# Ten probability tiles a pair through device memory in place of eight, five differences of them on GpSimd, and new instruction orders

## What is computed

```python
Q = (x @ Wq.T).reshape(b, n, H, R)          # H = 8, R = 64
K = (x @ Wk.T).reshape(b, n, H, R)
V = (x @ Wv.T).reshape(b, n, H, d)          # d = 128
attn = jax.nn.softmax(jnp.einsum('bnhr,bmhr->bhnm', Q, K), axis=-1)
out = jnp.einsum('bhnm,bmhd->bnd', attn, V) # summed over the heads
x = _layernorm(x + out)
h = jax.nn.silu(_tlin(x, w1_w, w1_s)) * _tlin(x, w2_w, w2_s)
h = gelu(_tlin(h, h1_w, h1_s)); h = gelu(_tlin(h, h2_w, h2_s))
x = _layernorm(x + _tlin(h, w3_w, w3_s))
```

## Time and profile before

| | |
|---|---|
| median of three executions | 941.37 us (940.90 to 941.87) |
| the profiled execution | 942.06 us, with a span of 940.3 us from the first to the last instruction |
| period of a pair, steady | 56.7 us |
| PE busy | 915.1 us, 97% |
| ACT busy | 841.1 us, 89% |
| DVE busy | 819.9 us, 87% |
| POOL busy | 590.4 us, 63% |
| mean granted TensorE clock | 0.994 |

### The profile page before, as it was taken

One profiled execution on the slowest core, in us unless ns is written; L12 is line 12 of the kernel. 1 busy time (PEld: TensorE's weight loads), 2 busy tenths in 40 slices (PEclk: granted clock), 3 DMA queues, 4 the chain that ended last, 5 costly groups with the idle time before them and its releaser, 6 DMA issues.

```text
span 940.3 us, 19462 instructions
## 1 busy us (share of the span) xinstructions
PE 915.1 (97%) x6071; PEld 766.8 (82%) x6071; DVE 819.9 (87%) x1786; ACT 841.1 (89%) x2081; POOL 590.4 (63%) x587
## 2 busy tenths in 40 slices
PE   8989999999999999999999999999999999999996
PEld 6887888878888888888888888888888888888886
DVE  7999698897989989898897989989898897987767
ACT  7969998999989899999999999999999999989963
POOL 7954655748567485665847557485665747565753
PEclk9999999999999999999999999999999999999998
DMA  6005042241423315143151423415143141420010
GB/s 205 13 22 171 13 144 82 76 138 46 149 66 112 115 32 169 47 141 96 49 155 53 150 69 92 129 39 160 55 135 102 49 152 49 132 82 23 24 35 25
DMA packets 113640, 84.49 MB, mean 90 GB/s; under 512 B 11264, under 2 KB 93824, under 8 KB 113536
## 3 DMA queue, kind: packets, MB, share of 16 engines
q1 hardware_dynamic: 113536, 83.22, 28.3%
HBM read 45.69 MB, written 37.49 MB: 88 GB/s over the span
## 4 chain that ended last, share of the span: by engine, by line
PE 63%; DVE 16%; ACT 9%; DMA 5%; issue 5%; SPq 1%; POOL 1%; POOLq 0%; DVEq 0%; ACTq 0%
PE bank L1717 11%; PE bank L1718 11%; PE bank L1584 9%; PE bank L1585 7%; PE bank L1586 7%; PE bank L1590 7%; PE bank L1644 7%; ACT prob L661 6%; DVE pt_lo L316 4%; DVE t_lo L316 2%; DVE neg_max L1086 2%; DMA crossing<-prob 2%; DMA pt_lo<-crossing 2%; DVE gated L1170 2%; DVE gated L1162 2%
## 5 line engine op out<-in xcount | busy, mean ns | idle before, releaser
L440 POOL TENSOR_TENSOR prob<-prob,inv_total 128x512 f32<-128x512 f32 x256 | 264.1, 1042 | 133.0 <-DVE inv_total L1092 133.0
L661 ACT ACTIVATE prob<-bank,neg_max 128x256 f32<-128x256 f32 x512 | 238.6, 489 | 29.6 <-DVE neg_max L1086 27.7
L1086 DVE TENSOR_REDUCE neg_max<-bank 128x2 f32<-128x512 f32 x256 | 168.7, 669 | 9.5 <-PE bank L1644 9.5
L316 POOL TENSOR_TENSOR odd_lo<-gated,odd_hi 128x512 fp32r<-128x512 f32 (+1 forms) x64 | 80.7, 1262 | 128.9 <-ACT odd_hi L319 128.9
L1584 PE MATMUL bank<-pt_hi,v_hi 128*128 128x256 f32 x512 | 156.8, 306 | 2.5 <-DVE pt_lo L316 2.0
L316 DVE TENSOR_TENSOR pt_lo<-bank,pt_hi 128x512 fp32r<-128x512 f32 x144 | 98.1, 683 | 53.1 <-ACT pt_hi L319 51.6
L1585 PE MATMUL bank<-pt_lo,v_hi 128*128 128x256 f32 x512 | 144.2, 282 | 0.0
L1586 PE MATMUL bank<-pt_hi,v_lo 128*128 128x256 f32 x512 | 144.1, 282 | 0.0
L1584 PEld LDWEIGHTS bank<-pt_hi,v_hi 128*128 128x128 f32 x512 | 96.6, 189 | 27.8 <-DVE pt_lo L316 23.3
L661 ACT ACTIVATION_READ_ACCUMULATOR prob<-bank,neg_max 128x1 f32 x512 | 112.9, 221 | 0.0
L316 DVE TENSOR_TENSOR pt_lo<-pt_lo,pt_hi 128x512 fp32r<-128x512 f32 x112 | 100.5, 897 | 5.6 <-ACT pt_hi L319 5.4
(11 more groups left out here) (153 smaller groups left out, 2601.0 us busy)
## 6 DMA issues: line engine op xcount, KB each, us to landing
crossing<-prob SPq DMA_DIRECT2D x112, 256.0 KB, 2.2
pt_lo<-crossing SPq DMA_DIRECT2D x448, 64.0 KB, 2.1
xt_in<-in_x_t SPq DMA_DIRECT2D x16, 256.0 KB, 3.3
res<-in_x SPq DMA_DIRECT2D x16, 256.0 KB, 2.9
passing<-y SPq DMA_DIRECT2D x15, 256.0 KB, 2.0
yt<-passing SPq DMA_DIRECT2D x60, 64.0 KB, 2.0
out_x<-y SPq DMA_DIRECT2D x15, 256.0 KB, 2.3
h_in<-in_h_t SPq DMA_DIRECT2D x2, 1024.0 KB, 9.2
```

Of the source, the lines that this page charges most:

```text
L316: return eng.tensor_tensor(dst, src, hi.bitcast(F32), ALU.subtract)
L440: nc.gpsimd.tensor_tensor(tile, tile, by, ALU.mult).then_inc(s_norm, 1)
L661: last = nc.scalar.activation(into, scored, ACT.Exp, bias=neg_max[:, u, nt:nt + 1], accum_out=total[:, u, nt:nt + 1])
L1086: nc.vector.tensor_reduce(neg_max[:, u, :], sc_bank(i, u).rearrange("p (t m) -> p t m", m=N), AX.X, ALU.max, negate=True).then_inc(s_max, 1)
```

## The change

Tiles 12 and 13 of the pairs 1 to 14 go through device memory too, and for the tiles 4, 6, 8, 10 and 12 of these pairs the low part is made by GpSimd. The step lists of all five engines, in the head, the period and the tail, and the bank tables are new. All other differences of the text follow from these.

```diff
-SENT = (4, 5, 6, 7, 8, 9, 10, 11)
+SENT = (4, 5, 6, 7, 8, 9, 10, 11, 12, 13)
+POOLED = (4, 6, 8, 10, 12)
...
+    def pooled(i, u):
+
+        return u in POOLED and 0 < i < LAST
...
+    def lows_to(i, u):
+
+        return i * J + u + 1 - pooled_to(i, u)
...
+            def pt_low(i, u):
+                if there(i):
+                    pool.wait_ge(s_pt_hi, after(i, J, u + 1))
+                    s = slot(i, u, 4)
+                    minus(nc.gpsimd, whole(pt_lo, s), whole(pt_lo, s).bitcast(F32), whole(pt_hi, s)).then_inc(s_pl_lo, 1)
...
-                    pe.wait_ge(s_pt_lo, after(i, J, u + 1))
+                    if pooled(i, u):
+                        pe.wait_ge(s_pl_lo, pooled_to(i, u))
+                    else:
+                        pe.wait_ge(s_pt_lo, lows_to(i, u))
...
                 norm(k, 9)
+                low(k - 2, 3, 1)
+                pt_low(k, 4)
                 norm(k, 10)
+                norm(k, 11)
+                norm(k, 12)
+                pt_low(k, 6)
+                low(k - 2, 3, 2)
+                low(k - 2, 3, 3)
                 low(k - 1, 1, 0)
+                pt_low(k, 8)
+                norm(k, 13)
                 low(k - 1, 1, 1)
-                norm(k, 11)
+                pt_low(k, 10)
...
-                prob_out(k, 11)
+                prob_out(k, 11)
+                prob_out(k, 12)
...
+                prob_out(k, 13)
+                prob_back(k, 12)
+                prob_back(k, 13)
```

More of the change, by code:

```diff
@@ L53 @@
[L53 to L59, removed]
@@ new lines, in _ @@
+                gelu3(k - 2, 2)
+                pt_high(k, 6)
+                gelu3(k - 2, 3)
+                high(k - 2, 3, 2)
+                t_high(k + 1, 3)
+                high(k - 1, 1, 0)
+                high(k - 2, 3, 3)
+                v_high(k, 6)
+                tanh(k - 1, 1)
+                exp(k, 14)
+                t_high(k + 1, 4)
+                pt_high(k, 7)
+                pt_high(k, 8)
+                tanh(k - 1, 2)
+                yt_copy(k - 2)
+                v_high(k, 7)
@@ new lines, in _ @@
+            largest_low(6)
+            v_low(0, 5)
+            row_max(0, 12)
+            inverse(0, 10)
+            t_low(1, 1)
+            row_max(0, 13)
+            pt_low(0, 6)
+            t_low(1, 2)
+            inverse(0, 11)
+            v_low(0, 6)
+            v_low(0, 7)
+            largest_low(3)
+            inverse(0, 12)
+            t_low(1, 3)
+            pt_low(0, 7)
+            t_low(1, 4)
+            pt_low(0, 8)
+            row_max(0, 14)
+            row_max(0, 15)
@@ new lines, in _ @@
+                inverse(k, 11)
+                norm2(k - 3)
+                turn_prob_blocks(k, 9)
+                turn_prob_blocks(k, 10)
+                pt_low(k, 5)
+                t_low(k + 1, 2)
+                inverse(k, 12)
+                gate(k - 1, 0)
+                turn_prob_blocks(k, 11)
+                t_low(k + 1, 3)
+                row_max(k, 14)
+                v_low(k, 6)
+                turn_prob_blocks(k, 12)
+                silu(k - 1, 1)
+                row_max(k, 15)
@@ L1510, in _ @@
-            stats2_of(13)
-            inverse(15, 15)
-            pt_low(15, 12)
-            x1t_low_half(0)
-            norm2(13)
             pt_low(15, 13)
@@ new lines, in cycle @@
+                    scores(k, 5, (s_gelu3, k - 2, KC, 2), (s_pt_lo, k, J, 4))
+                    times_v(k, 0)
+                    times_v(k, 1)
+                    turn_x1(k - 1, (s_v_lo, k, VT, 5))
+                    times_v(k, 2)
+                    layer3(k - 2, 2, 0, w, (s_exp, k, J, 8))
+                    times_v(k, 3)
+                if k == 1:
+                    query_or_key(k + 1, 0, (s_x1, k - 1, 2, 2))
+                else:
+                    query_or_key(k + 1, 0, (s_x1t_lo, k - 1, 1, 1))
@@ L2156, in _ @@
-            turn_prob(1, 1, (s_t_lo, 1, H, 7))
-            values(1, 1, (s_pt_lo, 0, J, 13))
-            turn_attention(0, 0, (s_exp, 1, J, 5))
-            times_v(0, 14)
+            turn_prob(1, 1, (s_pt_lo, 0, J, 16))
             times_v(0, 15)
```

1112 lines of the change are left out of this document (535 added, 577 removed), and 3 rows, old and new, of the table TURN_OTHER.

## The result

The changed kernel takes **928.28 us** (median of four executions, 927.12 to 929.71); the kernel before took 941.13 us beside it (940.33 to 941.87). The ratio is 0.9864, with a 95% interval of 0.9845 to 0.9884: faster by 12.9 us, where 11.8 were predicted. The profiled execution took 927.26 us with a span of 925.1, so 14.8 us less than that of before, and the median 12.9: executions of one kernel lie up to 2.6 us apart here, and both traces are single ones. One execution of a later run (the kernel with the later `y_add`) took 3018 us and stands in no median here.

The account below looks back on a forecast made before the run. PE was taken as the bound, busy 56.13 of 56.60 us a period. Terms -12.3 + 5.3 - 6.2 + 4.2 - 1.5 - 2.5 + 1.2 = -11.8 us gave 929.6 us as the median, range 923.5 to 940.5.

Parts of the forecast that it names:

- The transposes, -12.3: PE, 14 periods: two turn_prob leave each, 28 tiles at 0.44 us, 12.3 us off PE.
- The seventh run of scores, +5.3: PE, 14 periods: seven runs of scores instead of six, each 0.38 us beyond its work, 5.3 us more.
- The waits that go, -6.2: PE, in the periods: waits for DVE's t_low ahead of scores(k, 6) taken as gone, 6.2 us.
- the new ones, +4.2: PE, in the periods: what is left of several tight margins, rated 0.3 us a period, 4.2 us; bounds 0 and 7.
- makes PE no faster by itself: DVE, in the periods: its lighter load makes its part of the path faster but gives PE nothing by itself.
- about 3 us a period: DVE, each period: 4.5 us less for differences, 1.4 us more for block transposes, about 3 us less.
- The head, -1.5 and -2.5: Head: 1.5 us from tiles 0 and 1 scaled before large weights; 2.5 us from an earlier t_low(1, 7) and the clock.
- The tail, +1.2: Tail: norm2(14) waits for rstd2_of(14) behind POOL's last low part, 1.2 us on the end (0 to 2.5).
- the spare of 1.3 us: ACT, each period: its list from start to start about 53.9 us against PE's 55.2, so about 1.3 us to spare.
- The third rival (ACT the bound): ACT, two added table loads a period: ACT becomes the bound, 949 us or, keeping all idle time, 974; chance 0.12.
- only PE's list: Whole kernel: only PE's shorter list counts, waits move elsewhere in the same amount, head gives nothing: 935.6 us; chance 0.22.
- held up by POOL and ACT: Periods: late ACT delays POOL's differences and what follows, PE loses about 0.8 us more a period: 941 us; chance 0.09.

Follow-up runs that it names:

- the kernel with the later `y_add`: Changed kernel with y_add(k - 3) four steps and stats2_of(k - 3) some six steps later in DVE's list: 929.95 us, ratio 0.9894.
- eight-load kernel: Changed kernel with a single-column gelu added between exp(k, 9) and exp(k, 10) in every period, two table loads more: 968.12 us, ratio 1.0280.

## Why the prediction was right

The sum was right to 1.3 us at the median, and 3.3 us too small against the profiled execution. The direction and its source, PE's shorter list with waits that go, were right; that the number came out so near is partly luck, since two errors cancel. By the sum a period is 0.64 us shorter (0.50 of list, 0.14 of waits), 5.8 us for the nine steady ones, and all the rest of the kernel gives 6.0. In the traces the nine steady periods give 15.6 us (1.73 each), and all the rest takes 0.5 more. Term by term:

- **The transposes, -12.3.** Right. `prob` has 464 transposes in place of 576, and two tiles are worth 0.87 us where nothing waits.
- **The seventh run of scores, +5.3.** The price is right (0.39 against 0.38); one run taken off again gives back 0.15 a period only, since PE's time follows PE's list only as long as the others keep up.
- **The waits that go, -6.2, and the new ones, +4.2.** This is the mis-sized step. I counted the idle time that the view of waits names, and rated new ones at 0.3 us a period. In the steady periods there are none: nine of them with 0.0 us of idle time where 4.9 were before. And more went than this: the nine periods fell by 1.73 us in the mean, of which the list is 0.50 and the idle time 0.54. The other 0.69 was in small waits inside PE's busy time. The weights' side shows them, as a wait for `pt_lo` that the changed kernel's list of waits no longer has among its largest:

```profile
PEld bank L1584 <- DVE pt_lo L316: 23.3, 66, 1.0
```

  In a steady period before, `times_v` came or took 0.1 to 0.3 us longer at four places, 0.7 us in all, behind a late `pt_lo`; from start to start the first of these matmuls stands 0.37 behind the one before it and 0.22 ahead of the next, where it is 0.23 and 0.12 without a wait:

```profile
484.93 0.40 PE L1718 MATMUL bank<-odd_lo,h_hi 128*128 128x512 f32 x1
485.30 0.39 PE L1584 MATMUL bank<-pt_hi,v_hi 128*128 128x256 f32 x1
485.52 0.28 PE L1585 MATMUL bank<-pt_lo,v_hi 128*128 128x256 f32 x1
```

  With POOL making half the differences of the tiles from memory, they are gone. That DVE's relief "makes PE no faster by itself" was thus wrong: with all differences on DVE the changed kernel is 17 us slower, in the better of the two orders tried. The relief itself was smaller than "about 3 us a period": DVE's busy time fell from 50.65 to 48.91 us a period, 1.7. New waits of about 4.2 us do exist, in a place that I had not named: 4.5 us come off the median when the two added table loads do, and in the traces 2.8 in the first four periods.
- **The head, -1.5 and -2.5.** The clock part came: from 60 to 70 us it is 1.00 where it was 0.83, and the wait of 2.39 us for `t_low` is gone. The waits did not fall with it: PE's idle time to the end of the first period is 8.3 us after and 7.9 before. The largest new one is DVE's, whose list has the maxima over the weights' low parts in this place:

```profile
48.38 0.63 PE L1618 MATMUL bank<-ident,prob 128*128 128x128 f32 x4 [1.50 <-DVE pt_lo L332]
```

  So some 1.7 us of the 4.0 came, by the clock (an estimate: 0.17 of 10 us), and new waits took them back. The wait for POOL at 18.6 us did go. The step that failed is "I take 1.5 us" for POOL's order, without a look at who is late next.
- **The tail, +1.2.** Right in its cause, too small: 2.7. `norm2(14)` waited 1.69 us for `rstd`, and 1.1 us of its own stand on the path.
- **ACT.** Its table loads are 86 as foreseen, its busy time 54.5 a period (54.5 to 55.3), POOL's 42.8 (about 42). But the spare of 1.3 us, from adding up the steps from start to start, was an error of about 1.2: the eight-load kernel shows none. The busy time, which I had set aside as counting run-outs, was the better guide: with 0.5 us of idle time in a period ACT is full. The third rival (ACT the bound) was therefore nearer than its 0.12: in the steady periods ACT's added loads cost only 0.08 us, but two more raise the period by their whole length.

Of the rivals, "only PE's list" (935.6) and "held up by POOL and ACT" (941) did not come. The rule of the Trainium skill on two-input elementwise work (GPSIMD Engine Reference, Engine selection) holds in the direction of its price (it says about twice; here POOL takes 1.31 us for such a difference and DVE 0.83 in the mean, 1.6 times) and not in what would follow for this kernel: moving five a period to the slower engine is worth 17 us, since PE waits for DVE's results (15.8 us in three groups of waits in the run above) and, behind its first 2 us, has no wait for POOL in its list of waits in the changed kernel.

```profile
L332 DVE TENSOR_TENSOR pt_lo<-pt_lo,pt_hi 128x512 fp32r<-128x512 f32 x70 | 58.0, 829 | 37.0 <-ACT pt_hi L335 37.0
L332 POOL TENSOR_TENSOR pt_lo<-pt_lo,pt_hi 128x512 fp32r<-128x512 f32 x70 | 91.5, 1307 | 35.6 <-ACT pt_hi L335 35.5
```

## What to carry to other kernels

When one engine is full, count its waits in the distances of its instructions too, not only in its idle time, and ask for each engine that feeds it how late its results are: work given to a slower engine that nobody waits for can be worth much, though it takes nothing off the bound engine. Removing one wait alone shows what is behind it (here 1.6 us came off for one priced at 6.2), so price a wait by what is late next. When a sum comes out right, compare it stretch by stretch as well: here two errors of some 6 to 10 us hid in it. And take an engine's busy time at its word when you ask for room: add one known cost to it, as the two table loads here, and see what the period does.

## What was not expected of the hardware

- A wait of PE can cost more than itself, through the clock. In the eight-load kernel PE waited 1.94 us for ACT's exps, and the granted clock of 192 to 194 us was 0.50, all of it at the lower of its two levels:

```profile
191.13 0.50 PE L1614 MATMUL bank<-wv_hi,xt_hi 128*128 128x512 f32 x1 [1.94 <-ACT prob L693]
```
```profile
192.00:194.00 2.00, 2.00 (x6) 1.57 (x6) 1.40 (x4) 2.00 (x5) 0.35 (x1) 0.50 0.59 141
```

- It does not always do so. The eight-load kernel has 13 such waits, all of 1.94 to 1.95 us; four of them have a fall of the clock behind them, and these periods take 58.4 to 58.8 us, most of the others 57.96 to 58.00. In the kernel with the later `y_add` two waits of 0.78 and 0.93 us (at 893.5 and 894.9) came just ahead of the 0.50 from 896 on; the changed kernel has the same two waits, 0.79 and 0.93 us at 891.9 and 893.3, and no such fall behind them in its trace. Of its four executions the two with a mean granted clock of 0.995 took 927.1 and 927.3 us, those with 0.994 and 0.993 took 929.7 and 929.3. That these had the fall in this place is an inference: only one execution has a trace. What the fall costs here is 1.0 us, by the three traces that have it.
- How long DVE takes for a difference of two SBUF tiles goes with whether POOL is at work. The changed kernel's 70 differences `pt_lo<-pt_lo,pt_hi` on DVE have two lengths and nothing in between: 56 take 0.64 to 0.70 us, among them all 42 beside which POOL is idle, and the 14 that POOL's work covers from end to end take 1.45 in the mean. Two of them, and what POOL does beside the first (it does nothing beside the second):

```profile
484.34 1.48 DVE L332 TENSOR_TENSOR pt_lo<-pt_lo,pt_hi 128x512 fp32r<-128x512 f32 x1
479.13 0.67 DVE L332 TENSOR_TENSOR pt_lo<-pt_lo,pt_hi 128x512 fp32r<-128x512 f32 x1
484.23 3.49 POOL L460 TENSOR_TENSOR prob<-prob,inv_total 128x512 f32<-128x512 f32 x3
```

  The same difference from a PSUM bank takes 0.68 us in either case. In the kernel before, 42 of 112 were long ones, three a period in place of one, so its mean of 0.90 us is a mixture, and what moving one of them saves depends on which.
- `norm2`, four instructions on DVE, took 1.11 us at 916.6 in the tail, where POOL was idle, and 1.82 us in a period (the row with `y<-y,mv,rstd` above, 480.65).
